# Pixel attention on one core: a step ordered by the form of its products, maxima over contiguous queries, and a small transpose for the rows

## The reference

```
xn   = group_norm(x, 32 groups)
q, k, v = einsum('oc,bct->bot', w_qkv, xn) + b_qkv      # 8 heads of 32 channels
weight  = softmax(einsum('bct,bcs->bts', q, k) / sqrt(32))   # 1024 x 1024 for each head
a    = einsum('bts,bcs->bct', weight, v)
x    = x + w_proj a + b_proj
```

## Time and profile before

| | |
|---|---|
| median of the runs | 2230.95 us (2216.08 to 2231.27) |
| the profiled execution's own time | 2227.61 us |
| its span | 2225.8 us |
| busy share PE, DVE, ACT, POOL | 89%, 69%, 37%, 46% |
| the chain that ended last | PE 71%, DVE 16%, issue 4%, DMA 4% |
| mean granted clock of TensorE | 0.935 |

### The profile page before, as it was taken

One profiled execution on the slowest core, in us unless ns is written; L12 is line 12 of the kernel. 1 busy time (PEld: TensorE's weight loads), 2 busy tenths in 40 slices (PEclk: granted clock), 3 DMA queues, 4 the chain that ended last, 5 costly groups with the idle time before them and its releaser, 6 DMA issues.

```text
span 2225.8 us, 36373 instructions
## 1 busy us (share of the span) xinstructions
PE 1979.0 (89%) x12212; PEld 1015.5 (46%) x12212; DVE 1531.2 (69%) x2315; ACT 827.0 (37%) x1546; POOL 1029.1 (46%) x437
## 2 busy tenths in 40 slices
PE   6999685799999999999999999999999969888885
PEld 2443232354554554544544544545544335445442
DVE  6766647787666777676777766777666127888786
ACT  0152310004544544443544443544545613333320
POOL 0243210005455355454454444454444608788787
PEclk8799888789999999999999999999999979999996
DMA  7200020232330330330330330330331020122211
GB/s 219 58 2 1 1 85 27 57 115 62 77 77 20 78 79 21 77 79 20 77 79 20 77 79 20 77 79 20 78 77 39 2 97 25 63 65 66 79 46 60
DMA packets 89664, 132.53 MB, mean 60 GB/s; under 512 B 58180, under 2 KB 58486, under 8 KB 89462
## 3 DMA queue, kind: packets, MB, share of 16 engines
q1 hardware_dynamic: 79958, 129.36, 21.1%
q10 hardware_dynamic: 9504, 0.59, 0.3%
HBM read 44.83 MB, written 25.17 MB: 31 GB/s over the span
## 4 chain that ended last, share of the span: by engine, by line
PE 71%; DVE 16%; issue 4%; DMA 4%; ACT 2%; SPq 2%; POOL 1%; POOLq 0%; DVEq 0%; ACTq 0%
PE AV L650 11%; PE S L637 11%; PE RB L621 11%; PE S L621 5%; PE SUM L660 4%; PE RB L689 4%; PE RB L885 3%; DVE MX L1276 3%; SPq L443 2%; PE AV L898 2%; PE RB L766 2%; DVE ENC L1617 2%; DVE DEV L1316 2%; PE RB L706 2%; PE RB L934 1%
## 5 line engine op out<-in xcount | busy, mean ns | idle before, releaser
L1276 DVE TENSOR_REDUCE MX<-RB 128x1 f32<-128x512 f32 x783 | 515.2, 684 | 89.3 <-PE RB L621 80.7
L1014 ACT ACTIVATE PR<-S 128x512 f32<-128x512 f32 x640 | 356.5, 597 | 578.3 <-PE S L637 559.0
L1175 POOL TENSOR_TENSOR ACC<-PR 128x1024 f32<-128x1024 f32 x72 | 170.3, 2373 | 760.6 <-ACT PR L1014 758.7
L637 PE MATMUL S<-QS,KS 98*128 98x512 f32 x1152 | 470.2, 460 | 17.4 <-issue 8.5
L1175 POOL TENSOR_TENSOR ACC<-ACC,PR 128x1024 f32<-128x1024 f32 x152 | 360.0, 2371 | 198.2 <-ACT PR L1014 189.4
L621 PE MATMUL RB<-KS,QS 96*128 96x512 f32 x783 | 393.1, 524 | 32.7 <-DVE MX L1276 20.1
L1014 ACT ACTIVATE X<-S 128x512 f32<-128x512 f32 x512 | 283.7, 597 | 284.0 <-PE S L637 277.2
L621 PEld LDWEIGHTS RB<-KS,QS 96*128 96x128 f32 x783 | 245.0, 318 | 251.6 <-DVE MX L1276 153.0
L637 PEld LDWEIGHTS S<-QS,KS 98*128 98x128 f32 x1152 | 222.4, 198 | 218.5 <-issue 93.6
L1276 DVE TENSOR_REDUCE MX<-S 128x1 f32<-128x512 f32 x369 | 251.7, 682 | 32.2 <-PE S L621 27.0
L621 PE MATMUL S<-KS,QS 96*128 96x512 f32 x369 | 186.3, 505 | 11.4 <-DVE MX L1276 6.8
(11 more groups left out here) (235 smaller groups left out, 2096.3 us busy)
## 6 DMA issues: line engine op xcount, KB each, us to landing
X<-out_y SPq DMA_DIRECT2D x24, 1024.0 KB, 5.1
QS<-HI SPq DMA_DIRECT2D x144, 128.0 KB, 2.4
KS<-HI SPq DMA_DIRECT2D x144, 128.0 KB, 2.5
out_y<-X SPq DMA_DIRECT2D x16, 1024.0 KB, 4.1
QS<-LO SPq DMA_DIRECT2D x72, 128.0 KB, 2.6
KS<-LO SPq DMA_DIRECT2D x72, 128.0 KB, 2.4
X<-in_x SPq DMA_DIRECT2D x8, 1024.0 KB, 8.7
OHU<-out_y SPq DMA_DIRECT2D x8, 512.0 KB, 4.4
```

Of the source, the lines that this page charges most:

```text
L637: mm(ST[:, (H * s + h) % BANKS, :], KS[par][:, h, P * mt:P * mt + P], QS[par][:, h, HALF * half:HALF * half + HALF], start=True, stop=True ...
L1014: nc.scalar.activation(exps(i, s, pair)[:, HALF * one:HALF * one + HALF], ST[:, (H * s + h) % BANKS, :], ACT.Exp, scale=1.0 if i is None e ...
L1175: nc.gpsimd.tensor_tensor(ACC[:, pair, :], so_far, exps(i, s, pair), ALU.add).then_inc(pool_used, 1)
L1276: nc.vector.tensor_reduce(out=MX[:, h, t, half:half + 1], in_=bank(), op=ALU.max, axis=AX.X).then_inc(ring_free, 1)
```

## The change

Two kinds of jobs are told apart in a step. PE now issues each score followed by one maximum, the rest of the maxima after the fourth score, then the values of the step before, then all other jobs, then the sums. VectorE does a step's maxima first and its other jobs last. Group t of the maxima is now queries 128 t to 128 t + 127, so the weights are contiguous. NM for a head is then in the wrong order, and a new job ("flip", h) transposes it on TensorE into 8 x 128 through the ring; VectorE makes NMH and NML from that bank, and a row transfer consists of eight pieces of 128 values. The flip stands in the step behind the one with the head's last maximum, and for that the maxima are laid into steps 1 to 13 only. By the planner, a short window (Q/K and V jobs, spreads) then has 0, 5, 6, 6, 6, 5, 6, 6, 6, 4, 4, 4, 4, 2, 0, 0 maxima in its steps (before: 0, 4, 5, 5, 5, 4, 5, 5, 5, 3, 3, 3, 3, 4, 5, 5), and a long one (output products, statistics and group sums besides) 0, 1, 7, 6, 7, 5, 5, 5, 7, 4, 4, 4, 4, 5, 0, 0 (before: 0, 0, 6, 5, 6, 4, 4, 4, 6, 3, 3, 3, 3, 5, 6, 6). Before windows 0 and 2 flips stand in START and first_jobs, the last one of first_jobs behind four Q/K products.

```diff
-        steps = range(1, STEPS)
+        steps = range(1, STEPS - 2)
 ...
+        done = [s for s in range(STEPS) for job in jobs[s] if job[0] == "max" and job[2:] == (MT - 1, 1)]
+        for h, s in enumerate(done):
+            jobs[s + 1].append(("flip", h))
     return jobs
+def maxima_of(jobs):
+    return [job for job in jobs if job[0] == "max"]
+def others(jobs):
+    return [job for job in jobs if job[0] != "max"]
 ...
     START += [[("v", 1)], [("qk", 0, 0)], [("qk", 0, 1), ("qk", 1, 0)], [("qk", 1, 1)]][_h]
+    START += [("flip", _h)]
 ...
-    maxima = [("max", h, t, half) for h in range(H) for t in range(MT) for half in range(2)]
+    maxima = []
+    for h in range(H):
+        maxima += [("max", h, t, half) for t in range(MT) for half in range(2)] + [("flip", h)]
 ...
-    return jobs, maxima + [("qk", n // 2, n % 2, 1) for n in range(4)]
+    return jobs, maxima[:-1] + [("qk", n // 2, n % 2, 1) for n in range(4)] + maxima[-1:]
 ...
-        NMH = sb("NMH", [P, H, MT], f32r)
-        NML = sb("NML", [P, H, MT], f32r)
+        NMH = sb("NMH", [MT, H, P], f32r)
+        NML = sb("NML", [MT, H, P], f32r)
 ...
-                        load(QS[par][r:r + 1, h, :].rearrange("o (p t) -> o p t", t=MT).bitcast(f32),
+                        load(QS[par][r:r + 1, h, :].rearrange("o (t p) -> o t p", p=P).bitcast(f32),
                              src[:, h, :].bitcast(f32), rows_in[h])
 ...
-                mm(bank(), QS[par][0:3 * D, h, t:N:MT], KS[par][0:3 * D, h, HALF * half:HALF * half + HALF],
+                mm(bank(), QS[par][0:3 * D, h, P * t:P * t + P], KS[par][0:3 * D, h, HALF * half:HALF * half + HALF],
                    start=True, stop=True).then_inc(ring_full, 1)
+            def flip(u, h):
+                dst = bank()
+                wait(pe, max_ready, H * u + h + 1)
+                nc.tensor.transpose(dst[0:MT, 0:P], NM[:, h, :], IDENT).then_inc(ring_full, 1)
 ...
                 for s in range(STEPS):
-                    scores(u, par, s, (0,))
-                    run(jobs[s][0:1])
-                    scores(u, par, s, (1, 2))
-                    run(jobs[s][1:3])
+                    todo = maxima_of(jobs[s])
+                    for h in range(H):
+                        scores(u, par, s, (h,))
+                        run(todo[h:h + 1] if h < H - 1 else todo[h:])
                     if s:
                         values(u, par, s - 1, i)
                     elif trail:
                         values(u - 1, 1 - par, STEPS - 1, i)
-                    run(jobs[s][3:4])
-                    scores(u, par, s, (3,))
-                    run(jobs[s][4:5])
+                    run(others(jobs[s]))
                     if s:
                         sums(u, s - 1, i)
                     elif trail:
                         sums(u - 1, STEPS - 1, i)
-                    run(jobs[s][5:])
 ...
-                    wait(dve, rows_in[h], 2 * 16 * u)
-                    link(nc.vector.tensor_reduce(out=NM[:, h, :], in_=MX[:, h], op=ALU.max, axis=AX.X,
-                                                 negate=True))
-                    link(nc.vector.tensor_copy(NMH[:, h, :], NM[:, h, :]))
-                    nc.vector.tensor_tensor(NML[:, h, :], NM[:, h, :], NMH[:, h, :].bitcast(f32),
-                                            ALU.subtract).then_inc(negmax_ready, 1)
+                    nc.vector.tensor_reduce(out=NM[:, h, :], in_=MX[:, h], op=ALU.max, axis=AX.X,
+                                            negate=True).then_inc(max_ready, 1)
+            def flip(u, h):
+                src = bank()[0:MT, 0:P]
+                wait(dve, rows_in[h], 2 * 16 * u)
+                link(nc.vector.tensor_copy(NMH[:, h, :], src))
+                nc.vector.tensor_tensor(NML[:, h, :], src, NMH[:, h, :].bitcast(f32),
+                                        ALU.subtract).then_inc(ring_free, 1)
+                own()
+                dve.sem_inc(negmax_ready, 1)
 ...
                 for s in range(STEPS):
-                    run(jobs[s][0:3])
+                    run(maxima_of(jobs[s]))
                     if s == (1 if par == 1 and i is None else INVERT_AT) and trail:
                         invert(2 * u - 1)
                     if s == MT + INVERT_AT:
                         invert(2 * u)
-                    run(jobs[s][3:])
+                    run(others(jobs[s]))
```

More of the change, by code:

```diff
@@ L348, in program @@
         v_ready = sem("v_ready")
+        max_ready = sem("max_ready")
         negmax_ready = sem("negmax_ready")
@@ L409, in iteration @@
             window(u + 1, 1, window_jobs(prep=not last, nxt=not last, gn=last), i)
-        RING_PER = 2 + 2 + 4 + 2 + 4 + 64 + 2 + 2 + 4 + 64
+        RING_PER = 2 + 2 + 4 + 2 + 4 + 64 + H + 2 + 2 + 4 + 64 + H
         TURNS = B - 2
@@ L721, in run @@
                             max_scores(u + 1, 1 - par, *job[1:])
+                        elif job[0] == "flip":
+                            flip(u + 1, job[1])
                         elif job[0] == "v" and i is None:
@@ L833, in prepare @@
                         max_scores(2, 0, *job[1:])
+                    elif job[0] == "flip":
+                        flip(2, job[1])
             pe.wait_ge(scaled, 1)
@@ L849, in _ @@
                     qk_l0(1, job[1], job[2])
+                elif job[0] == "flip":
+                    flip(0, job[1])
                 else:
@@ L1541, in _ @@
                 ring.enter(i - 1, RING_PER)
-                steps.enter(i - 1, 8 + 16 + 6)
+                steps.enter(i - 1, 8 + 16 + 6 - 2 * H)
                 iteration(i, window, None)
```

## The result

The changed kernel takes **2404.81 us** in the median (2402.39 to 2410.47) against 2231.11 us: a ratio of 1.080, 95% interval 1.075 to 1.085. The forecast had the direction and less than half of the size, +60 of some +178 us, and its range ended at 2335. In the profiled executions the span went from 2225.8 to 2408.7 us.

The account below looks back on a forecast made before the run. TensorE's order was taken to set the pace, VectorE having slack on average only. Seven short windows at +5.1, eight long at +2.0, plus 3 and 5, gave +60 on 2227.6: 2288 us, range 2253 to 2335.

Parts of the forecast that it names:

- The step from sum to forecast: Summed step times for new windows, 81.1 and 91.5 us, set against the old measured 76.0 and 89.5: +5.1 and +2.0.
- The ring (part 2): Maxima in a burst wait for VectorE to free three banks: steps with 4, 5, 6, 7 take 3.10, 3.55, 4.15, 4.75 us.
- part 3: Steps 14, 15 and 0, without maxima: the fourth score waits for the first's exponential, 2.60 us instead of 2.35.
- rival (a): VectorE's slack absorbs the bursts and only TensorE's own order counts: -98 us, 2130; chance 0.15.
- The edge kept at 1.9 (part 6): The wait at the loop's edge stays 1.90 us; it may fall to 1.0, leaving 5 us as a lower end.
- The clock (rival c): New stalls of 4 us in step 2 bring one more 1.2 GHz stretch per window: +26 us, 2314; chance 0.13.
- The statistics (part 4): In long windows the statistics fall between V part 1 and step 2's first maximum; that step takes 8.55 us, not 4.75.
- The lag of Q/K products: Splits behind the values delay the next step's maxima: 3.80 us instead of 3.10, three times a window.
- One-offs and window 0: Flips behind Q/K work before windows 0 and 2 cost 2 and 3 us; window 0, of sixes, costs 3.
- The cast (part 6): The maxima's cast reads PSUM, so its stalls go; if still blocked, at most 1.55 us twice a window; taken as 0.
- (b): Burst costs and removed stalls cancel over the kernel: +4 us, about 2231; chance 0.17.
- (d): The flip waits for the maxima, 4 x 0.7 us a window: +42 us, 2330; chance 0.02.

Follow-up runs that it names:

- f: Changed kernel with each maximum taken over 256 of the 512 keys of its product: 2296.7 us, ratio 1.033.
- j: Changed kernel with 196 more satisfied wait instructions at TensorE's start: 2400.0 us, ratio 1.077.
- m: Changed kernel with one maxima product computed 13 times in step 2 of a long window, during TensorE's wait behind the statistics: 2363.3 us, ratio 1.060.
- i: Kernel before with 60 more instructions of satisfied waits at TensorE's start, nothing else: 2252.7 us, ratio 1.012.
- c: Changed kernel with SP loading the next image only once the four scores of step 0 are made: 2417.9 us, ratio 1.088.
- g: Changed kernel with the old walk through a step, and the next image loaded only after the first score of the loop's first window: 2261.5 us, ratio 1.017.
- d: Changed kernel with the statistics moved from step 1 to step 0, ahead of the V product's copy: 2346.9 us, ratio 1.054.
- o: Changed kernel with statistics in step 0, 196 more satisfied waits at TensorE's start, and maxima over 256 of 512 keys: 2240.9 us, ratio 1.006.
- e: Changed kernel with a step's other products right behind its first score, and VectorE's part of them ahead of the maxima: 2397.2 us, ratio 1.078.
- a: Changed kernel with the old walk through a step on TensorE and VectorE; contiguous queries, flips and 13 steps stay: 2270.4 us, ratio 1.019.
- b: Kernel before with only the new walk through a step; strided queries, no flips, maxima in steps 1 to 15: 2412.6 us, ratio 1.085.
- p: Kernel before with each maximum over 256 of 512 keys: 2197.4 us, ratio 0.986.
- h: Changed kernel with the old walk through a step, the next image loaded two windows' halves earlier, and statistics in step 0: 2240.3 us, ratio 1.009.

## Why the prediction was wrong

The short and the long window were forecast at 81.1 + 91.5 = 172.6 us and took 87.7 + 101.0 = 188.7. By intervals between value blocks, one pass (forecasts by the prediction's terms; a V, Q/K or residual product 1.7, a second block 0.89):

| interval | forecast | measured | over |
|---|---|---|---|
| the loop's edge | 2.60 + 0.89 + 1.90 = 5.4 | 9.78 | 4.4 |
| the step after it, half clock | 3.7 + 1.7 + 2 x 0.89 = 7.2 | 9.77 | 2.6 |
| statistics | 8.55 + 1.7 = 10.25 | 10.67 | 0.4 |
| the two steps behind, mostly half clock | 4.15 + 5.0 = 9.15 | 6.43 + 6.37 | 3.7 |
| eight steps with Q/K products | 44.9 | 48.2 | 3.3 |
| the 19 others | 95.7 | 97.5 | 1.8 |

- **The step from sum to forecast: wrong.** I set a bare sum for the new order against the measured time of the old one. By the same terms the windows before come to 53.0 + 19.0 + 1.9 = 73.9 and 53.0 + 19.0 + 6.8 + 0.5 = 79.3 us, 12.3 us a pass under the measured 76.0 and 89.5. That rest (in one long window waits for MX of 0.56, 0.21, 0.78 and 1.49 us, two slow stretches and more) was thereby taken as gone. Sum against sum gives +7.2 and +12.2 a window and, worked out afterwards, 7 x 7.2 + 8 x 12.2 + 8 = +156, an estimate of 2384 us, where 2404.8 was measured. The table's rows say in which intervals the new kernel lies over its sum.
- **The ring (part 2): right.** 4.14 us for six maxima, 2.70 for none (969.90 to 972.60; forecast 2.60). So was part 3, and rival (a) falls by f.
- **The edge kept at 1.9 (part 6): wrong, the largest row.** I had weighed only whether it shrinks. It became 2.09 + 3.73 us, with half the clock behind it: 7.0 of 16.1 us a pass. Without the second wait the two intervals are 5.7 us shorter in the same turn of j and 6.1 in m. The mechanism was on no list: where the loop's code lies (i, j), and the load of XIN, which I had not put at the edge and which stretches the waits (c, g). The changed kernel has some 60 TensorE instructions more ahead of its loop, 20 flips with their waits, and i shows that 60 are enough; that it was the flips is not isolated.
- **The clock (rival c): right in kind, too small.** I gave it 0.13 as an extra of one stretch a window, 26 us, and only behind the statistics. It fell behind the edge and behind the statistics, 2.6 us over the forecast there and 3.1 us here, the latter as 6.43 - 4.15 (d) and 6.37 - 5.58 (m). Rival and forecast were one case: once I had costed a wait of 4 us in step 2, the half clock behind it belonged into the sum.
- **The statistics (part 4): the step itself 10.67 against 10.25.** d and o confirm it as a loss of the walk.
- **The lag of Q/K products: 0.4 us a step too small.** A product held for LO (0.4 to 0.8 us of idle time) comes with a late fourth score. e did not separate it.
- **One-offs and window 0: 8 us forecast, 21 measured** up to the first value block of window 2, and windows 2 and 3 took 19 us more (7 forecast). That block starts at 506.0 us in a and at 509.7 in b, 7.7 and 11.3 us later than before: layout, flips and 13 steps seem to hold one part of the 21 us and the walk the other, by one execution each.
- **The cast (part 6): right.** It never blocks now (my bound for one that does, 1.55 us, was read from one cast; the longest took 4.15). By its line (ns min/median/max), answering to the earlier trace rows:

```profile
L1312 DVE CAST NMH<-RB x46: 268/279/280, 78.4 to 1879.7; 8x128 fp32r<-8x128 f32 x46
L1312 DVE CAST NMH<-S x26: 217/279/280, 47.4 to 1888.8; 8x128 fp32r<-8x128 f32 x26
```

  Its maximum is 280 ns where it was 4154. That a two-port VectorE operation and a GpSimd operation lock each other out is the Trainium skill's rule ("SBUF — State Buffer", SBUF: two separate sides); with PSUM as the source no lock-out shows. Shape and place of the cast changed with its source, and no run tells them apart.
- Rivals (b) and (d) are out: the stalls that went did not cancel the rest, and the flip follows its block after 1.00 us without waiting.

On the Trainium skill's rule that I cited for (c), that TensorE's clock oscillates when it cycles through PSUM banks with micro-idles ("TensorE: Matmul & The Clock Gate", A second HAM failure mode: psum-queue depth-cycling): the trace doesn't bear it out for idle times of 0.2 us. Steps of six maxima, held at the ring each time, ran at 1.06 us a value block. The clock fell behind the waits of 3.47 and 3.73 us in every turn, and at two places of the loop (value blocks of 1.67 and 1.71 us at 1225.24 and 1604.16) behind waits of 0.72 to 0.83 us for LO, so short ones were not always harmless.

No version beat the kernel before but p, which leaves half of the keys out. Open are the loss ahead of the loop, the price of the Q/K lag by itself, the share of the half clock alone, and what TensorE waits for in the second wait.

## What to carry to other kernels

Put the sum for the old order, by the same terms, beside its measured time before a new one is forecast; what the terms leave over doesn't go away by itself. Interleaving is what lets a ring of three banks carry an engine that is busy 70% of the time; grouping by form saves about 0.2 us a step on TensorE (a step of five maxima takes 4.14 us in f with a SUM block of 0.89 in it, so 3.25 without it, and 3.47 in p) and turns the other engine's average slack into waits. Where a forecast contains a new wait of some microseconds on TensorE, put the half clock behind it into the sum, twice the time of what follows for a block or two. And a change of the instruction count ahead of a loop can itself be worth 1% at the loop's edge: look at the first microseconds of a pass before and after, and pad one kernel as a control before the order is blamed.

## What was not expected of the hardware

- 60 instructions of satisfied waits ahead of a loop added a wait of 1.5 to 2.1 us behind each of its edges (i); 196 more took such a wait of 3.7 to 4.3 us away (j) and cost 8 us themselves. In the old walk, with XIN's load beside the edge its two waits made 6.3 to 7.0 us together (a), with that load elsewhere 3.8 to 4.6 (h).
- 12 superfluous products a pass made the kernel 41 us faster (m), most of it at the loop's edge, where the second wait was gone.
- Weight loads of 128 contiguous queries take 203 ns, those with a stride of eight took 318; the pace between products stayed at 0.24 us either way, as forecast.
